# Value bias through the output projection, V copied out by ScalarE, a contiguous residual sum, one-launch maxima, and another order of steps

## The chip, the core and the metric

One NeuronCore of a Trainium2 chip runs the whole program. The metric is the device time of one execution in microseconds (us). Engines are named as in the profile: PE (TensorE), DVE (VectorE), ACT (ScalarE), POOL (GpSimd), SP (SyncE, which here only issues DMAs).

## What is computed

A decoder layer with three parts, each followed by a layer norm, on x of 8 sequences by 128 tokens by 512 features, in float32:

```
x = layernorm(x + self_attention(x))       # 32 heads of 16, qkv and output projections with biases
x = layernorm(x + cross_attention(x, ctx)) # 32 query heads on 8 key/value heads, ctx 8x128x128, additive mask
x = layernorm(x + ffn(x))                  # router softmax over 8 experts scales inputs and outputs of one sign(weight) matmul
# self-attention, as in the reference:
qkv = x @ attn_qkvw + attn_qkvb
probs = softmax(q @ k.T / sqrt(16)); ctx = probs @ v
return ctx @ attn_ow + attn_ob
```

## The kernel before

The eight sequences are worked on in four pairs, i = 0 to 3, each with sequences b = 0 and 1. Three threads of steps are woven into one list, `ORDER`: thread A is self-attention, B is cross-attention and the FFN, C is the set-up of the weights. A token such as `B2.s:0,3` is thread B, pair 2, step `s`, sequence 0, group 3. Every engine walks the same list and does its own part of each step, so the list fixes the order on each engine's queue; across engines only semaphores order the work. The list was written out as a table. PSUM is two rings of banks, one for thread A and one for B and C (class `Ring`): three banks of each rotate over the steps, the fourth is for `pv`. A step on PE waits until the bank it gets has been emptied.

Products that need float32 precision are made of high and low parts: `project` issues three matmuls for each of four slices (`L877` to `L879`). Steps of thread A, in their order of work: `lc`/`xb` load c_in and x_in and make xb = x + output bias on POOL (`L495`); `xt` transposes x; `q:0` to `q:3` make the parts of q and k, each split by ACT (`L575`), DVE (`L695`, `L700`) and POOL (`L501`) and stored to DRAM by SP; `ldq`, `ldk` load them back in a stacked layout (`L336`); `v` projects V, and DVE adds the value bias while it copies it out of PSUM (`L707`); `s` makes scores, of which DVE takes the row maxima (`L713`); `mt` splits those maxima on POOL (`L470` to `L476`), transposes them on PE (`L934`), copies them out on DVE (`L719`) and has SP write them into three rows of the q tile by three DMAs (`L419`); `st` makes the scores transposed with the maxima subtracted (`L943`), ACT takes exp (`L587`); `pv` multiplies by V (`L956`); `ot`, `ct`, `op` normalise, transpose and project (`L738` adds xb to the projection's PSUM bank on DVE), `n1` is the norm. The columns of the features are kept in another order after the norm ("tile-permuted": within each of four tiles, dimension before head), so `L738` writes with a stride.

Thread B has the same steps on the other side: `cp`, `ctx`, `ldc` for the keys, `xt`, `ldx` for the queries, `s` with maxima of score plus mask. Here DVE does one fused operation for each of four 128-column pieces of a bank (`L777`), which writes a full 128x128 result, that nobody reads, over `x2`, and its minimum to `nmb`. From the second group on it first waits for its own previous group to be done:

```
if g > 0:
    rb.wait_emptied(dve, i, "s", b, g - 1)
```

Then follow `st` (`L1010`, `L1011`, `L1013`, exp `L595`), `pv` (`L1021`), `ot`, `n2`, `cx`, and the router and FFN (`rl`, `rt`, `rr`, `is`, `os`, `ff`, `n3`). Set-up steps of thread C: `small` (biases and gate weights), `w` (split of the qkv weight), `ow` (ACT makes owH, `L659`, POOL makes owL, `L550`), `sign`/`swt`, `mask`, `scales`, `rows`.

Of the kernel before, what the change touches and what calls it, by code (L numbers as in the profile page):

```python
# [40 lines left out]
def steps(table):  # L41
# [14 lines left out]
    C0.swt:2 A0.st:1,0 A0.ot:0,1 A0.st:1,1 A0.st:1,2 A0.pv:1,0 A0.ct:0 A0.pv:1,1 A0.pv:1,2 C0.swt:0 A0.st:1,3 C0.rows
    B0.ldc:0 A0.st:1,4 A0.op:0 A0.pv:1,3 A0.st:1,5 A0.st:1,6 A0.pv:1,4 A0.st:1,7 A0.pv:1,5 A0.pv:1,6 A0.pv:1,7 A0.n1:0
    A0.ot:1,0 B0.ldc:1 B0.xt:0 B0.ldx:0 A0.ot:1,1 A1.q:0 A0.ct:1 A1.q:1 A1.q:2 A1.ldq:0 A1.q:3 A0.op:1 B0.s:0,0 A1.v:0
    B0.s:0,1 B0.s:0,2 B0.s:0,3 B0.s:0,4 A1.ldk:0 B0.s:0,5 B0.s:0,6 B0.s:0,7 A1.ldq:1 A0.n1:1 A1.v:1 B0.mt:0 A1.s:0,0
    A1.s:0,1 A1.s:0,2 A1.ldk:1 A1.s:0,3 A1.s:0,4 B0.xt:1 A1.s:0,5 A1.s:0,6 A1.s:0,7 B0.ldx:1 B0.st:0,0 B0.st:0,1  # L60
# [1043 lines left out]
```

## Time and profile before

| | us |
|---|---|
| median of 3 runs | 401.22 (400.49 to 401.77) |
| the profiled execution, its own time | 400.77 |
| its span, first to last instruction | 399.0 |
| PE busy in the span | 336.9 (84%) |
| DVE busy | 263.7 (66%) |
| ACT, POOL busy | 154.5 (39%), 113.2 (28%) |

Matmuls are pipelined and their ends are modelled, so busy PE is not PE at its peak. The granted clock (PEclk) is the share of TensorE's full speed that the throttle let through; a mean of 0.5 in a stretch is its lower level throughout.

### The profile page before, as it was taken

What the parts mean: (1) busy time and instruction counts of PE and PEld (TensorE: products, weight loads), DVE (VectorE), ACT (ScalarE), POOL (GpSimd) and SP (SyncE); (2) the same over time, 40 slices, a digit from 0 to 9 for tenths busy, and PEclk for the clock granted to TensorE, in tenths of its full rate; (3) what the DMA queues carried; (4) which work ended last, traced back from release to release, by engine and by line L of the source; (5) the groups of instructions that cost most, each with busy time, mean ns of one, the idle gap of its engine ahead of it and who ended that gap; (6) DMA issues with size and microseconds to landing.
All of it is one profiled execution on the core that took longest, in us unless ns stands there. A gap on an engine that the chain in (4) does not pass through costs nothing.

```text
span 399.0 us, 7582 instructions
## 1 busy us (share of the span) xinstructions
PE 336.9 (84%) x2661; PEld 240.7 (60%) x2661; DVE 263.7 (66%) x942; ACT 154.5 (39%) x301; POOL 113.2 (28%) x203
## 2 busy tenths in 40 slices
PE   1693789997889999997999999969999977599583
PEld 1692556795647767975567579756556654344251
DVE  1977744558856747698786477977963776933525
ACT  3942145420144854302277642122556611036330
POOL 3363400131240214432432044253022243000231
PEclk9998559998895999997999999967999996569858
DMA  7969700268570000785620016767100053300001
GB/s 270 382 187 250 170 5 5 69 186 222 147 189 4 14 21 25 224 231 145 177 71 2 3 44 194 233 147 194 36 17 1 2 142 109 92 3 2 0 0 53
DMA packets 26702, 42.58 MB, mean 107 GB/s; under 512 B 8153, under 2 KB 18529, under 8 KB 24361
## 3 DMA queue, kind: packets, MB, share of 16 engines
q1 hardware_dynamic: 26393, 41.58, 37.1%
q8 instruction: 21, 0.34, 0.4%
q10 hardware_dynamic: 272, 0.52, 0.3%
q14 instruction: 16, 0.13, 0.1%
HBM read 29.32 MB, written 12.32 MB: 104 GB/s over the span
## 4 chain that ended last, share of the span: by engine, by line
PE 64%; DVE 20%; DMA 5%; issue 4%; ACT 2%; POOL 2%; SPq 2%; POOLq 0%; DVEq 0%; ACTq 0%
DVE x L777 8%; PE bank_a L877 7%; PE bank_a L879 6%; PE bank_a L878 6%; PE bank_a L956 4%; PE bank_a L926 4%; PE bank_b L1021 4%; PE bank_b L1010 4%; PE bank_a L943 3%; PE bank_b L1013 3%; PE bank_b L1011 3%; DVE nma L713 3%; PE bank_b L1056 2%; PE bank_b L1057 2%; PE bank_b L998 2%
## 5 line engine op out<-in xcount | busy, mean ns | idle before, releaser
L777 DVE CUSTOM_DVE_ANT_0 x<-bank_b,mraw 128x128 f32<-128x128 f32 x256 | 59.0, 286 | 8.6 <-PE bank_b L998 2.5
L595 ACT ACTIVATE pb<-bank_b 128x512 f32<-128x512 f32 x64 | 37.6, 600 | 59.7 <-PE bank_b L1013 42.5
L587 ACT ACTIVATE pa<-bank_a 128x512 f32<-128x512 f32 x64 | 37.5, 597 | 25.6 <-PE bank_a L943 13.5
L713 DVE TENSOR_REDUCE nma<-bank_a 128x4 f32<-128x512 f32 x64 | 39.9, 681 | 6.4 <-PE bank_a L926 6.2
L877 PE MATMUL bank_a<-xH,wH 128*128 128x256 f32 x128 | 37.2, 290 | 3.4 <-DVE xL L685 3.4
L1010 PE MATMUL bank_b<-idr,mH 128*128 128x512 f32 x64 | 36.2, 566 | 0.6 <-DVE nmb L777 0.5
L878 PE MATMUL bank_a<-xL,wH 128*128 128x256 f32 x128 | 36.5, 286 | 0.0
L879 PE MATMUL bank_a<-xH,wL 128*128 128x256 f32 x128 | 36.5, 285 | 0.0
L998 PE MATMUL bank_b<-kx,qx 96*128 96x128 bf16 x256 | 26.9, 252 | 11.0 <-DVE nmb L777 8.2
L926 PE MATMUL bank_a<-ks,qs 96*128 96x128 bf16 x256 | 25.2, 250 | 10.6 <-DMA ks<-scr_k 8.4
L998 PEld LDWEIGHTS bank_b<-kx,qx 96*128 96x128 bf16 x256 | 18.4, 112 | 20.4 <-DVE nmb L777 12.4
L926 PEld LDWEIGHTS bank_a<-ks,qs 96*128 96x128 bf16 x256 | 18.8, 112 | 18.4 <-issue 10.3
L956 PE MATMUL bank_a<-pa,va 128*32 128x128 f32 x512 | 27.2, 309 | 0.9 <-ACT wide_a L602 0.4
L877 PEld LDWEIGHTS bank_a<-xH,wH 128*128 128x128 f32 x128 | 24.8, 194 | 3.9 <-DVE xL L685 3.8
L1011 PE MATMUL bank_b<-idr,mL 128*128 128x512 f32 x64 | 26.2, 409 | 0.0
L1013 PE MATMUL bank_b<-qx,kx 99*128 99x512 bf16 x64 | 26.1, 408 | 0.0
L943 PE MATMUL bank_a<-qs,ks 99*128 99x128 bf16 x256 | 25.2, 242 | 0.9 <-DVE nma L713 0.9
L878 PEld LDWEIGHTS bank_a<-xL,wH 128*128 128x128 f32 x128 | 24.8, 194 | 0.0
L879 PEld LDWEIGHTS bank_a<-xH,wL 128*128 128x128 f32 x128 | 24.7, 193 | 0.0
L943 PEld LDWEIGHTS bank_a<-qs,ks 99*128 99x128 bf16 x256 | 17.7, 108 | 8.8 <-issue 6.8
L777 DVE DVE_READ_ACCUMULATOR2_ANT nmb<- 128x1 f32 x256 | 21.1, 82 | 0.0
L481 POOL TENSOR_SCALAR rsb<-mvb 128x1 f32<-128x1 f32 x16 | 3.8, 235 | 58.3 <-DVE mvb L673 58.3
(159 smaller groups left out, 728.3 us busy)
## 6 DMA issues: line engine op xcount, KB each, us to landing
wraw<-in_L_attn_attn_qkvw_dram SPq DMA_DIRECT2D x3, 1024.0 KB, 8.6
scr_q<-qp SPq DMA_DIRECT2D x8, 384.0 KB, 3.1
qs<-scr_q SPq DMA_DIRECT2D x8, 384.0 KB, 4.5
scr_k<-kp SPq DMA_DIRECT2D x8, 384.0 KB, 4.2
ks<-scr_k SPq DMA_DIRECT2D x8, 384.0 KB, 4.8
scr_x<-xp SPq DMA_DIRECT2D x8, 384.0 KB, 2.6
qx<-scr_x SPq DMA_DIRECT2D x8, 384.0 KB, 4.3
qs<-scr_q SPq DMA_DIRECT2D x8, 256.0 KB, 4.7
```

Source lines behind the costliest of these rows:

```text
L713: dve.tensor_reduce(nma[:, b, 4 * j:4 * j + 4], pa_bank(i, *step)[:].rearrange("p (m t) -> p m t", m=KT), AX.X, ALU.max, negate=True).then ...
L777: last = dve.tensor_tensor_reduce(x2[:, b, r * P:(r + 1) * P], pb_bank(i, *step)[:, r * P:(r + 1) * P], mraw[:], -1.0, -LOWEST, ALU.add, A ...
L877: pe.matmul(dst, lh, rh, start=kt == 0, stop=False)
L878: pe.matmul(dst, lh, rl_, start=False, stop=False)
L879: last = pe.matmul(dst, ll, rh, start=False, stop=kt == KT - 1)
L926: last = pe.matmul(dst[:, m * P:(m + 1) * P], qs[0:SR, b, j, m, :], ks[0:SR, b, j, m, :], start=True, stop=True)
L943: last = pe.matmul(dst[:, m * P:(m + 1) * P], ks[0:SM, b, j, m, :], qs[0:SM, b, j, m, :], start=True, stop=True)
L956: last = pe.matmul(dst[m * VW:(m + 1) * VW, (j % 4) * P:(j % 4 + 1) * P], va[:, b, j * KT + m, :], pa[:, n % NP, m * P:(m + 1) * P], start ...
L998: last = pe.matmul(dst[:, r * P:(r + 1) * P], qx[0:SR, b, 4 * (g % 2) + r, g // 2, :], kx[0:SR, b, g, :], start=True, stop=True)
L1010: pe.matmul(d4, mH[:], ident4, start=True, stop=False)
L1011: pe.matmul(d4, mL[:], ident4, start=False, stop=False)
L1013: pe.matmul(d4, kx[0:SM, b, g, :], qx[0:SM, b, a:a + 4, g // 2, :], start=False, stop=True).then_inc(*rb.is_full(i, *step))
```

## The change

1. The value bias is no longer added to V. As the probabilities of a row sum to one, it passes through the attention unchanged, so it is multiplied once by the output weight (a new step `C0.vb`, twelve 128x512 matmuls on PE with the bias column broadcast) and added once to the output bias by DVE. It is loaded as a 4x128 tile (`vraw`) and split in `scales`.
2. V is copied out of PSUM by ACT.
3. The columns of owH and owL are stored tile-permuted, xb is written tile-permuted by POOL, and the residual sum on DVE reads and writes contiguously.
4. The unread result of the fused maxima is written as bfloat16, so that two groups fit into `x2`, and each group waits for the one before the last instead of the last.
5. The three DMAs of a step `mt` become one.
6. `ORDER` is another list, with `C0.vb` added.

```diff
-    A0.lc C0.small C0.w:0 A0.xt:0 A0.xt:1 C0.w:1 C0.w:2 B0.cp:0 B0.cp:1 A1.lc A0.xb A0.q:0 C0.sign A0.q:1 A0.q:2
...
+    C0.small C0.w:0 A0.xt:0 A0.xt:1 C0.w:1 C0.w:2 A0.q:0 C0.sign A0.lc A0.q:1 A0.ldq:0 A0.q:2 C0.swt:3 A0.q:3 A0.ldk:0
...
+            sp.dma_start(vraw[:], qkvb[2 * H:3 * H].rearrange("(t p) -> t p", p=P)).then_inc(ld_small, 16)
-            sp.dma_start(vbias[:], qkvb[2 * H:3 * H].partition_broadcast(P)).then_inc(ld_vb, 16)
...
-                    for c in range(NPART):
-                        row = dst[SR + c:SR + c + 1, b]
-                        sp.dma_start(row.rearrange("r h m t -> r (h m) t"),
-                                     src[c * HEADS:(c + 1) * HEADS, b, :]).then_inc(done, 16)
+                    sp.dma_start(dst[SR:SM, b].rearrange("r h m t -> r (h m) t"), src[:, b, :]).then_inc(done, 16)
...
                     if i == 0:
-                        pool.wait_ge(ld_ob, 16)
+                        rb.wait_emptied(pool, 0, "vb")
...
-                        pool.tensor_tensor(xb[:, b, :], x_in[:, b, :], obias[:], ALU.add).then_inc(xb_made, 1)
+                        pool.tensor_tensor(by_dim(xb[:, b, :]), by_head(x_in[:, b, :]).rearrange("p m h d -> p m d h"),
+                                           by_head(obias[:]).rearrange("p m h d -> p m d h"), ALU.add).then_inc(xb_made, 1)
...
-                        pool.tensor_tensor(owL[:, kt, :], oraw[:, kt, :], owH[:, kt, :].bitcast(F32), ALU.subtract).then_inc(ow_low, 1)
+                        pool.tensor_tensor(by_dim(owL[:, kt, :]), by_head(oraw[:, kt, :]).rearrange("p m h d -> p m d h"),
+                                           by_dim(owH[:, kt, :].bitcast(F32)), ALU.subtract).then_inc(ow_low, 1)
...
+                elif thread == "A" and name == "v":
+                    b = step[1]
+                    ra.wait_full(act, i, *step)
...
+                    act.activation(va[:, b].rearrange("p (h m) w -> p m h w", m=KT)[:, :, :, 0:HD],
+                                   pa_bank(i, *step)[:].rearrange("p (m h d) -> p m h d", m=KT, d=HD), ACT.Copy).then_inc(*ra.is_empty(i, *step))
...
-                        act.activation(owH[:, kt, :], oraw[:, kt, :], ACT.Copy).then_inc(ow_high, 1)
+                        act.activation(by_dim(owH[:, kt, :]), by_head(oraw[:, kt, :]).rearrange("p m h d -> p m d h"), ACT.Copy).then_inc(ow_high, 1)
...
-                elif thread == "A" and name == "v":
...
-                    dve.tensor_tensor(va[:, b].rearrange("p (h m) w -> p m h w", m=KT)[:, :, :, 0:HD],
-                                      pa_bank(i, *step)[:].rearrange("p (m h d) -> p m h d", m=KT, d=HD),
-                                      vbias[:].rearrange("p (m h d) -> p m h d", m=KT, d=HD), ALU.add).then_inc(*ra.is_empty(i, *step))
...
-                    dve.tensor_tensor(tile_permuted(x1[:, b, :]), by_head(pa_bank(i, *step)[:]), by_head(xb[:, b, :]), ALU.add).then_inc(*ra.is_empty(i, *step))
+                    dve.tensor_tensor(x1[:, b, :], pa_bank(i, *step)[:], xb[:, b, :], ALU.add).then_inc(*ra.is_empty(i, *step))
...
-                    if g > 0:
-                        rb.wait_emptied(dve, i, "s", b, g - 1)
+                    unread = x2[:, b, :].bitcast(BF16)
+                    if g > 1:
+                        rb.wait_emptied(dve, i, "s", b, g - 2)
...
-                        last = dve.tensor_tensor_reduce(x2[:, b, r * P:(r + 1) * P], pb_bank(i, *step)[:, r * P:(r + 1) * P], mraw[:], -1.0, -LOWEST,
+                        part = 4 * (g % 2) + r
+                        last = dve.tensor_tensor_reduce(unread[:, part * P:(part + 1) * P], pb_bank(i, *step)[:, r * P:(r + 1) * P], mraw[:], -1.0, -LOWEST,
                                                         ALU.add, ALU.min, nmb[:, b, col:col + 1])
...
+                elif thread == "C" and name == "vb":
+                    rb.wait_full(dve, 0, "vb")
+                    dve.wait_ge(ld_ob, 16)
+                    dve.tensor_tensor(by_head(obias[:]), tile_permuted(pb_bank(i, "vb")[:]), by_head(obias[:]), ALU.add).then_inc(*rb.is_empty(i, "vb"))
                 elif thread == "C" and name == "scales":
+                    dve.wait_ge(vb_split, 1)
+                    dve.tensor_copy(vbH[:], bqk[:, 2 * KT:3 * KT]).then_inc(vb_split, 1)
+                    dve.wait_ge(vb_split, 2)
+                    dve.tensor_tensor(vbL[:], bqk[:, 2 * KT:3 * KT], vbH[:].bitcast(F32), ALU.subtract).then_inc(vb_split, 1)
...
+                elif thread == "C" and name == "vb":
+
+                    rb.wait_free(pe, 0, "vb")
+                    pe.wait_ge(vb_split, 3)
+                    pe.wait_ge(ow_low, KT)
+                    project(pb_bank(i, "vb")[:], lambda kt: (vbH[:, kt:kt + 1].broadcast_to([P, P]), vbL[:, kt:kt + 1].broadcast_to([P, P])),
+                            lambda kt: (owH[:, kt, :], owL[:, kt, :])).then_inc(*rb.is_full(i, "vb"))
```

The order on PE at the start, from the last matmul of the V projection to the first scores (`ks`, `qs` are the stacked keys and queries). Before:

```order
L878 MATMUL bank_a<-wL,xH 128x512
L879 MATMUL bank_a<-wH,xL 128x512
L990 MATMUL bank_b<-idf,c_perm 128x128 [waits c_permuted1]
L926 MATMUL bank_a<-ks,qs 128x128 [waits k_stacked0,q_stacked0,empty_a2]
L926 MATMUL bank_a<-ks,qs 128x128 x3
```

In the change, the first and last rows of the twelve of `vb` among them:

```order
L893 MATMUL bank_a<-wL,xH 128x512
L894 MATMUL bank_a<-wH,xL 128x512
L892 MATMUL bank_b<-owH,vbH 128x512 [waits ow_low,vb_split,empty_b2]
L893 MATMUL bank_b<-owL,vbH 128x512
...
L893 MATMUL bank_b<-owL,vbH 128x512
L894 MATMUL bank_b<-owH,vbL 128x512
L941 MATMUL bank_a<-ks,qs 128x128 [waits k_stacked0,q_stacked0,empty_a2]
```

The first scores now stand behind the bias product, and that behind POOL's four owL passes.

The order on POOL at the start, in the change (the q and k splits came last before, behind the context copies and xb; the owL passes came after both cp operations):

```order
L506 TENSOR_TENSOR qp<-wide_a,qp 128x2x256 [waits a_second] x2
L506 TENSOR_TENSOR kp<-wide_a,kp 128x2x256 [waits a_second] x2
L530 COPY c_perm<-c_in 128x128 [waits ones_b,c_loaded]
L531 COPY vx<-c_in 128x8x16
L530 COPY c_perm<-c_in 128x128 [waits ones_b,c_loaded]
L531 COPY vx<-c_in 128x8x16
L555 TENSOR_TENSOR owL<-oraw,owH 128x512 [waits ow_high]
L555 TENSOR_TENSOR owL<-oraw,owH 128x512 x3
L520 TENSOR_TENSOR cp<-rc,cp 128x128 [waits c_second0]
```

The owL passes moved ahead of the context's third parts, and behind the four context copies.

The order of SP's DMAs ahead of the last pair's cross-attention scores (`qx` queries, `kx` keys). Before:

```order
L370 DMA scr_x<-xp 128x3x512 [waits b_third0]
L336 DMA qx<-scr_x 48x4096 [waits ln_b0,x_stored0]
L336 DMA qx<-scr_x 32x4096
L336 DMA qx<-scr_x 16x4096
L336 DMA kx<-scr_c 48x1024 [waits pv_b,c_stored1]
L336 DMA kx<-scr_c 32x1024
L336 DMA kx<-scr_c 16x1024
L336 DMA kx<-scr_c 48x1024 [waits pv_b,c_stored0]
L336 DMA kx<-scr_c 32x1024
L336 DMA kx<-scr_c 16x1024
```

In the change:

```order
L388 DMA scr_c<-cp 128x3x128 [waits c_third0]
L342 DMA kx<-scr_c 48x1024 [waits pv_b,c_stored0]
L342 DMA kx<-scr_c 32x1024
L342 DMA kx<-scr_c 16x1024
L376 DMA scr_x<-xp 128x3x512 [waits b_third0]
L342 DMA qx<-scr_x 48x4096 [waits ln_b0,x_stored0]
L342 DMA qx<-scr_x 32x4096
L342 DMA qx<-scr_x 16x4096
```

The keys of sequence 0 are loaded before its queries are stored; those of sequence 1 come after.

## Rows read from the trace of the kernel before

**Rows 1.** The page: busy times of the engines, and the chain by line.

```profile
PE 336.9 (84%) x2661; PEld 240.7 (60%) x2661; DVE 263.7 (66%) x942; ACT 154.5 (39%) x301; POOL 113.2 (28%) x203
...
DVE x L777 8%; PE bank_a L877 7%; PE bank_a L879 6%; PE bank_a L878 6%; PE bank_a L956 4%; PE bank_a L926 4%; PE bank_b L1021 4%; PE bank_b L1010 4%; PE bank_a L943 3%; PE bank_b L1013 3%; PE bank_b L1011 3%; DVE nma L713 3%; PE bank_b L1056 2%; PE bank_b L1057 2%; PE bank_b L998 2%
```

**Rows 2.** Windows: start:end, length, busy PE, PEld, DVE, ACT, POOL, PEclk, DMA share, GB/s.

```profile
90.00:100.00 10.00, 7.42 (x49) 5.53 (x47) 9.02 (x60) 0.00 (x0) 1.52 (x3) 0.80 0.81 215
120.00:130.00 10.00, 10.00 (x107) 7.07 (x106) 7.18 (x62) 4.45 (x8) 0.00 (x0) 0.50 0.02 5
180.00:190.00 10.00, 7.39 (x46) 5.45 (x45) 8.09 (x28) 2.34 (x6) 2.38 (x5) 0.73 0.60 147
260.00:270.00 10.00, 6.87 (x42) 5.24 (x40) 7.50 (x31) 2.45 (x6) 4.39 (x8) 0.66 0.63 158
340.00:350.00 10.00, 5.51 (x39) 3.53 (x40) 8.97 (x77) 0.00 (x0) 0.92 (x4) 0.50 0.25 66
```

**Rows 3.** Timeline of DVE: a group's border, a sequence's border, the last piece.

```profile
98.49 0.28 DVE L777 CUSTOM_DVE_ANT_0 x<-bank_b,mraw 128x128 f32<-128x128 f32 x1
98.70 0.28 DVE L777 CUSTOM_DVE_ANT_0 x<-bank_b,mraw 128x128 f32<-128x128 f32 x1
99.14 0.29 DVE L777 CUSTOM_DVE_ANT_0 x<-bank_b,mraw 128x128 f32<-128x128 f32 x1
...
344.25 0.28 DVE L777 CUSTOM_DVE_ANT_0 x<-bank_b,mraw 128x128 f32<-128x128 f32 x1
344.51 0.29 DVE L777 CUSTOM_DVE_ANT_0 x<-bank_b,mraw 128x128 f32<-128x128 f32 x1
...
352.70 0.28 DVE L777 CUSTOM_DVE_ANT_0 x<-bank_b,mraw 128x128 f32<-128x128 f32 x1
```

**Rows 4.** Groups by line and shape: the operations moved or reshaped, and their like.

```profile
L707 DVE TENSOR_TENSOR va<-bank_a,vbias 128x512 f32<-128x512 f32 x8 | 5.5, 687 | 2.3 <-PE bank_a L879 2.2
L738 DVE TENSOR_TENSOR x<-bank_a,xb 128x512 f32<-128x512 f32 x8 | 8.9, 1118 | 7.2 <-PE bank_a L879 7.2
L731 DVE TENSOR_TENSOR cL<-bank_a,cH 128x512 fp32r<-128x512 f32 x8 | 5.5, 686 | 8.2 <-ACT cH L613 8.2
```

**Rows 5.** The last pair's start: DMA issues (KB, us to land), timelines of SP, PE.

```profile
qx<-scr_x SPq DMA_DIRECT2D x8, 384.0 KB, 4.3
...
323.95 1.78 SPq L336 DMA_DIRECT2D qx<-scr_x  x3
325.83 3.71 SPq L336 DMA_DIRECT2D kx<-scr_c  x6
...
331.58 1.15 PE L998 MATMUL bank_b<-kx,qx 96*128 96x128 bf16 x8 [0.35 <-DMA kx<-scr_c]
...
333.49 0.63 PE L1056 MATMUL bank_b<-swT,zH 128*128 128x512 f32 x1
333.91 0.63 PE L1057 MATMUL bank_b<-swT,zL 128*128 128x512 f32 x1
```

**Rows 6.** Timeline of the start: POOL, DVE and PE around the first scores.

```profile
29.65 1.16 POOL L501 TENSOR_TENSOR kp<-wide_a,kp 128x512 bf16<-128x512 f32 x1 [1.67 <-DVE kp L700]
38.50 4.93 POOL L550 TENSOR_TENSOR owL<-oraw,owH 128x512 fp32r<-128x512 f32 x4
...
41.53 4.36 PE L926 MATMUL bank_a<-ks,qs 96*128 96x128 bf16 x32 [8.39 <-DMA ks<-scr_k]
```

**Rows 7.** Timeline of POOL: context copies at the start and in a later pair.

```profile
14.54 0.94 POOL L525 COPY c_perm<-c_in 128x128 f32<-128x128 f32 x1 [10.11 <-DMA c_in<-in_ctx_dram]
16.40 1.15 POOL L525 COPY c_perm<-c_in 128x128 f32<-128x128 f32 x1
...
117.94 0.39 POOL L525 COPY c_perm<-c_in 128x128 f32<-128x128 f32 x1 [3.98 <-PE bank_b L1021]
118.27 0.29 POOL L526 COPY vx<-c_in 128x128 f32<-128x128 f32 x1
```

**Rows 8.** The tile mra: SP's issues, ns min/median/max, first and last start.

```profile
L419 SPq DMA_DIRECT2D qs<-mra x24: 502/590/1359, 49.5 to 289.6; - x24
```

More of the change, by code:

```diff
@@ L56 @@
[L56 to L60, printed above, removed]
@@ L96 @@
-    B3.st:1,4 B3.pv:1,0 B3.st:1,5 B3.st:1,6 B3.st:1,7 B3.ot:1,0 B3.n2:0 B3.pv:1,1 B3.cx:0 B3.ot:1,1 B3.rl:0 B3.rt:0
-    B3.n2:1 B3.cx:1 B3.rl:1 B3.rr:0 B3.rt:1 B3.is:0 B3.rr:1 B3.os:0 B3.is:1 B3.ff:0 B3.os:1 B3.ff:1 B3.n3:0 B3.n3:1
+    C0.small C0.w:0 A0.xt:0 A0.xt:1 C0.w:1 C0.w:2 A0.q:0 C0.sign A0.lc A0.q:1 A0.ldq:0 A0.q:2 C0.swt:3 A0.q:3 A0.ldk:0
+    A0.ldq:1 B0.cp:0 B0.cp:1 A0.ldk:1 C0.ow A0.v:1 C0.scales B0.ctx:0 C0.mask C0.swt:2 B0.ctx:1 A0.v:0 C0.vb A0.s:0,0
+    A0.s:0,1 A0.s:0,2 A0.s:0,3 A0.s:0,4 A0.s:0,5 A0.s:0,6 A0.s:0,7 C0.swt:0 C0.swt:1 A0.mt:0 A0.s:1,0 A0.s:1,1 A0.s:1,2
@@ new lines @@
+    A0.s:1,3 A0.st:0,0 A0.s:1,4 C0.rows A0.s:1,5 A0.st:0,1 A0.s:1,6 A1.lc A0.pv:0,0 A0.s:1,7 A0.xb A0.st:0,2 A0.pv:0,1
+    A0.st:0,3 A0.st:0,4 A0.pv:0,2 A0.pv:0,3 A0.mt:1 A0.st:0,5 B0.ldc:1 A0.st:0,6 A0.pv:0,4 A0.st:0,7 A0.pv:0,5 A1.xt:0
+    A0.pv:0,6 A0.pv:0,7 A0.st:1,0 A0.ot:0,0 A0.ot:0,1 A0.st:1,1 A0.st:1,2 A0.pv:1,0 A0.ct:0 A0.pv:1,1 A0.st:1,3
+    A0.st:1,4 A0.pv:1,2 A0.pv:1,3 A0.op:0 A0.st:1,5 A0.pv:1,4 A0.st:1,6 A0.st:1,7 A0.ot:1,0 B0.ldc:0 A0.n1:0 A0.pv:1,5
+    A1.xt:1 A0.pv:1,6 A0.pv:1,7 B0.xt:0 B0.ldx:0 A0.ot:1,1 A1.q:0 A1.q:1 A1.ldq:0 A0.ct:1 A1.q:2 A1.q:3 A1.ldk:0 A0.op:1
@@ L98 @@
+    B3.s:1,0 B3.s:1,1 B3.s:1,2 B3.mt:0 B3.s:1,3 B3.s:1,4 B3.s:1,5 B3.s:1,6 B3.s:1,7 B3.st:0,0 B3.st:0,1 B3.st:0,2
+    B3.st:0,3 B3.mt:1 B3.st:0,4 B3.pv:0,0 B3.st:0,5 B3.st:0,6 B3.st:0,7 B3.ot:0,0 B3.st:1,0 B3.pv:0,1 B3.st:1,1
+    B3.st:1,2 B3.st:1,3 B3.ot:0,1 B3.st:1,4 B3.pv:1,0 B3.st:1,5 B3.st:1,6 B3.st:1,7 B3.ot:1,0 B3.pv:1,1 B3.n2:0 B3.cx:0
+    B3.ot:1,1 B3.rl:0 B3.rt:0 B3.rr:0 B3.n2:1 B3.cx:1 B3.is:0 B3.rl:1 B3.rt:1 B3.rr:1 B3.os:0 B3.is:1 B3.ff:0 B3.os:1
+    B3.ff:1 B3.n3:0 B3.n3:1
 """)
@@ L165, in decoder_layer @@
         ocS = sb("ocS", [4 * E, H], F32R)
-        bqk = sb("bqk", [P, 2 * KT], F32)
-        vbias = sb("vbias", [P, H], F32)
+        bqk = sb("bqk", [P, 3 * KT], F32)
+        vbH = sb("vbH", [P, KT], F32R)
+        vbL = sb("vbL", [P, KT], F32R)
         obias = sb("obias", [P, H], F32)
@@ L304, in by_head, with by_dim @@
             return ap.rearrange("p (m h d) -> p m h d", m=KT, d=HD)
+        def by_dim(ap):
+            return ap.rearrange("p (m d h) -> p m d h", m=KT, d=HD)
         def tile_permuted(ap):
```

97 lines of the change are left out of this document (46 added, 51 removed).

## The prediction

> **What bounds the kernel now.** I read the page first: PE is busy 84% of the span, DVE 66%, and the largest single entry of the chain that ended last is DVE's fused maxima, 8% of 399 us, about 32 us [rows 1]. Neither engine bounds the whole. At the start PE waits 8.39 us for the reloaded keys, up to 41.53 [rows 6]. The windows show who bounds what after that [rows 2]. In each pair comes a stretch in which the maxima of both attentions fall together: DVE is busy 9.02 of 10 us at 90 to 100 while PE has 2.58 us idle; the same pattern costs PE 2.61 us at 180 to 190 and 3.13 us at 260 to 270. In the last pair there is no self-attention left to fill in, and PE is idle 4.49 us of the 10 at 340 to 350 with DVE at 8.97. Elsewhere PE is full. So DVE work is worth its time in those stretches, and nearly nothing outside them.
>
> The timeline of DVE then shows something inside its work [rows 3]. Pieces of one group start 0.21 us apart (98.49, 98.70). The next group's first piece starts 0.44 us after the last piece (98.70 to 99.14), although its scores are in. That border is where DVE waits for its own previous group. At 344.25 to 344.51 the border between two sequences, where there is no such wait, takes 0.26 us. So the wait costs about 0.2 us a border.
>
> **The change, part by part.**
>
> *The wait for the group before the last.* With the bfloat16 result, the semaphore waited for is one group (0.86 us) old. I take each border down from 0.44 to 0.22 us, a gain of 0.22 us. The fused operation reads PSUM and float32 either way, so its own 0.28 us I leave; bounds for its change of output type are 0 by the row of its like, nothing nearer being shown. In a dense stretch of the middle pairs six borders follow each other directly (others have another DVE operation between): 1.3 us.
>
> The Trainium skill, "VectorE: DVE Perf Modes", section "The DRAIN you can't avoid", says the opposite: eight copies with a semaphore after each took as long as eight with one at the end, so the semaphore costs nothing extra. By that, this part is worth zero. It is a rival below.
>
> *V out by ScalarE.* It takes 0.69 us from DVE eight times [rows 4], two of them in each dense stretch: 1.4 us. On ACT, idle for all of 90 to 100 us [rows 2], it hides; if ACT were busy with exp when V arrives, PE's bank would be held for one exp longer.
>
> *Contiguous residual.* 1.118 us becomes what the contiguous like takes, 0.686 us [rows 4], 0.43 us each, eight times; one of them falls in each dense stretch. The price is a strided sum on POOL, with two inputs read by stride. POOL is busy 28% and xb is needed much later, so it hides, except where the new list puts it directly ahead of the split of the maxima (pair 1): there it is covered by eight reductions of the scores.
>
> So a dense stretch of a middle pair loses 1.3 + 1.4 + 0.4 = 3.1 us of DVE. PE's idle time in the middle one is 2.61 us, and it can't gain more than it idles; I take 2.6 us for each of the three: **7.8 us**. Bounds: 1.8 without the border term, 3.1 with all of it.
>
> *The last pair.* From 331.58 [rows 5] to 352.98 us [rows 3] DVE works through the last sixteen groups, 64 pieces, with thirteen such borders: 13 x 0.22 = **2.9 us**, all on the path, since PE stands idle 4.49 us in the middle of it even at its lower clock, 0.50 granted [rows 2]. Its first scores wait for the keys of sequence 0, the last of six DMAs that SP issues at 325.83 for 3.71 us, behind three for the queries [rows 5]. In the new list those keys come first. Late next are the queries: the last of three is issued at about 325.1 and, with the usual 4.3 us to land [rows 5], is there at about 329.5, and PE has other steps to do before the scores until 331.2, so I take **1.2 us**, bounds 0.4 (the wait shown) to 3.7 (the issues).
>
> *One DMA for the maxima.* Two issues of 0.59 us less on SP [rows 8], sixteen times. The bytes are the same. It is on the path only where PE has nothing else while it waits for `st`: at the start. I take 1.2 us there and 0 elsewhere, where PE's other thread covers it (PE is 10.00 busy at 120 to 130, [rows 2]). A slower single DMA, spread over fewer transfers, would show in the same place; bound 1 us the other way.
>
> *The start, where the change costs.* One more small DMA ahead of the weights: the first split waits for it, 0.4 us. Then the bias product: the first scores stand behind it on PE, and it behind POOL. POOL ends the last key split at 30.81 [rows 6]. Four context copies follow: 1.4 us if quiet (0.39 and 0.29 each), 4.1 us if slowed as at the start, when DVE had two-input work beside them (0.94 to 1.15) [rows 7]; the new list has DVE's `scales` there, so I take 3 us: 33.8. The four owL passes took 4.93 us, 1.23 each [rows 6]. With one input by stride I add the difference of the strided copy to the plain one, 0.10 us for 128 columns, so 0.4 for 512: 4 x 1.66 = 6.6 us, up to 40.5. Twelve 128x512 matmuls after an idle PE, as the FFN's after the idle PE of the last pair, start 0.42 us apart [rows 5]: 5.1 us, up to 45.6, against 41.53 now. That is 4.1 us, and DVE's sum of the bias, like the strided 1.1 us, delays the first maxima by another 0.6. Bounds: 37.1 + 2.8 (full clock) = 39.9, so no delay at all; or 35 + 10 + 5.1 = 50.1, 8.6 us. Given back: 1.2 us by the single DMA, and 1.0 us because DVE has less ahead of the first `mt` copy: two casts instead of a cast and two subtractions of 0.69 us [rows 4] with their waits. Start: 0.4 + 4.1 + 0.6 - 1.2 - 1.0 = **+2.9 us**.
>
> On owL the Trainium skill, "GPSIMD Engine Reference", section "Performance pitfalls for Q7 kernels", gives +50% for reads with a step above 8 bytes. It would make a pass 1.85 us (an estimate from that page and the 1.23) and the start 0.8 us later than my sum; no row here shows a strided two-input pass.
>
> *Sum:* -7.8 - 2.9 - 1.2 + 2.9 = -9.0 us. The profiled execution has 400.77 us; the median of the runs is 0.45 higher. 401.22 - 9.0 = **392.2 us**. The rest of the new list moves steps by a few places where PE is full; I cost it at nothing, covered by PE's queue of the other thread. If that cover fails, new idle time of the size of the old (1 to 3 us a stretch) appears.
>
> **Rivals.**
> - *Borders are free* (the page's rule). For it: the measurement that the page reports. Against: the 0.26 us border without the wait. It takes 3 x 1.3 (of which 0.5 in all was capped anyway) and 2.9 us back: 392.2 + 6.3 = 398.5. Chance 0.08.
> - *Gains turn into other waits.* DVE comes earlier, but PE waits for reloads, whose DMA share is 0.81 in these stretches [rows 2], or for reordered steps. Half of the 7.8 and 2.9 goes: 397.5. For it: SP and the DMA engines are busiest there. Chance 0.15; the upper third of it is no change.
> - *The clock pays more.* Now 120 to 130 us runs at 0.50 granted with PE 10.00 busy [rows 2]: some 5 us lost. If the stalls shrink enough that the lower level doesn't follow, up to 5 us there and 2 us after 260: 386. Chance 0.19.
> - *Slower: POOL's strided passes hold the start.* If a strided two-input pass is slowed as the context copies were (1.15 against 0.39 us, times 2.9), it takes 3.6 us: 35 + 14.4 + 5.1 = 54.5, 13 us late, and xb's two passes ahead of the split in pair 1 stick out by 3. With 0.6 + 0.4 and the 2.2 given back that is 14.8 us against 11.9 gained: 404. It turns the sign from about 2.9 us a pass on. For it: DVE has two-input work beside POOL's at the start again. Against: the four owL passes took 1.23 each without such work beside them, and `scales` ends before they begin. Chance 0.12.
> - *Not as said:* the same-type neighbour rows mislead and nothing changes within 0.3%: 0.03.
>
> **How the numbers follow.** My forecast has 0.43, in its own range 388 to 396; it rests on borders and V, both on rows. 0.3% (1.2 us) is about what a measurement can tell from no change. Faster by more than that: 0.43 + 0.19 + 0.07 + 0.11 = 0.80; the same 0.07 (the last case and parts of two others); slower 0.13. The range runs from 384 (clock case, with a little more) to 402, leaving out most of the slower case.
>
> **What would show it.** Borders of `L777`'s successor at 0.22 us, and its groups at 0.86; PE idle in 90 to 120 below 3 us; V copies on ACT at about 0.6 us; the residual at 0.69; PE's first scores at 44 to 47 us, with the bias product right before; POOL's owL passes at 1.7 us; the last pair's scores some 9 us earlier. It is wrong if the borders stay at 0.44, if the first scores come later than 50 us, or if the span shrinks while the dense stretches don't.

## The result and the profile after

The changed kernel takes **415.91 us** (median of 4 runs, 413.12 to 417.69), the kernel before beside it 400.86: 1.037 times as long, 95% interval 1.030 to 1.043. The forecast was 392.2, the range 384 to 402; the sign was wrong, and so was the range. The profiled execution took 416.56 us, its span is 414.5 (before 400.77 and 399.0). Ratios, here and below, are of the fast runs alone against those of the kernel before beside them (two of e2's four and two of e11's six runs were slow), so they can differ by some us from what the medians give.

The page of the changed kernel: busy times, and two groups of section 5 (line, engine, operation, tiles, busy and mean ns, then the idle time before it and what ended it).

```profile
PE 340.8 (82%) x2674; PEld 241.3 (58%) x2674; DVE 258.5 (62%) x937; ACT 159.9 (39%) x309; POOL 120.8 (29%) x203
...
L784 DVE CUSTOM_DVE_ANT_0 x<-bank_b,mraw 128x128 bf16<-128x128 f32 x256 | 55.5, 287 | 12.5 <-DMA out_dram<-x 11.4
...
L1013 PE MATMUL bank_b<-kx,qx 96*128 96x128 bf16 x256 | 27.9, 255 | 23.4 <-DVE nmb L784 21.1
```

DVE has 5.2 us less to do than in [rows 1] and still everything ends later. The second line is new: before its maxima DVE sat idle 11.4 us for `out_dram`, the store of the layer's output. In the trace of before no instruction waits for that store. The third says who paid: PE waited 21.1 us for the maxima (`L998` in the kernel before: 8.2 us). Of the 15.5 us by which the span is longer, PE is busy for 3.9 and idle for 11.6. The mean granted clock of the two profiled executions is the same (0.885, before 0.881), so a lower clock is not the cause.

The groups of the moved and reshaped operations in the changed kernel, against [rows 4] and [rows 6]:

```profile
L590 ACT ACTIVATE va<-bank_a 128x512 f32<-128x512 f32 x8 | 4.8, 594 | 29.6 <-PE bank_a L894 29.6
...
L742 DVE TENSOR_TENSOR x<-bank_a,xb 128x512 f32<-128x512 f32 x8 | 5.5, 689 | 10.9 <-PE bank_a L894 10.9
...
L499 POOL TENSOR_TENSOR xb<-x_in,obias 128x512 f32<-128x512 f32 x8 | 15.7, 1979 | 0.0
L555 POOL TENSOR_TENSOR owL<-oraw,owH 128x512 fp32r<-128x512 f32 x4 | 7.2, 1838 | 0.0
```

V on ScalarE takes 0.59 us and the residual 0.69, as forecast. The strided passes on POOL take 1.84 us (`L555`, one input by stride) and 1.98 us (`L499`, both), where I took 1.66 for the first.

**Where it went.** I lay both traces side by side by the first write of `nmb` in each sequence, the first cross maximum (`L777`, now `L784`). In pair 0 it stands at 92.4 us before and 95.4 after: +3.0. The lag then stands at +5.4 (pair 0, sequence 1), +4.3 and +4.5 (pair 1), **+14.5** (pair 2, sequence 0, at 265.3), +13.5, **+17.5** (the last pair, at 350.2), +15.0 (its second sequence) and +15.5 at the end. Two jumps, then, and a slow loss beside them.

The timelines of SP and of DVE in the changed kernel at the first jump, and DVE's line at the second (start, duration, engine, line):

```profile
256.50 0.90 SPq L350 DMA_DIRECT2D scr_q<-qp  x2
259.09 1.77 SPq L342 DMA_DIRECT2D qs<-scr_q  x3
260.91 0.58 SPq L447 DMA_DIRECT2D out_dram<-x  x1
```

```profile
255.37 1.40 DVE L691 TENSOR_SCALAR x<-x,mvb,rsb 128x512 f32<-128x512 f32 x1
...
260.22 0.43 DVE L713 CAST kp<-wide_a 128x512 bf16<-128x512 f32 x1
265.08 0.29 DVE L784 CUSTOM_DVE_ANT_0 x<-bank_b,mraw 128x128 bf16<-128x128 f32 x1 [4.44 <-DMA out_dram<-x]
...
349.94 0.29 DVE L784 CUSTOM_DVE_ANT_0 x<-bank_b,mraw 128x128 bf16<-128x128 f32 x1 [4.77 <-DMA out_dram<-x]
```

The unread result of the maxima lies in `x2`, so a pair's first group of a sequence waits until the output of the pair before has been stored from there. In the new list the normalisation that makes this output stands behind the next pair's first query split, and SP issues the store behind the query stores and reloads: at 260.91. DVE is done with everything else at 260.65 and idles 4.44 us, and since it works in order, the maxima of the self-attention behind it wait as well. In the list before, SP issued the same store at 244.99, 5.6 us ahead of the maxima that need it.

DVE waits for the store three times: 2.21 us from 205.7, 4.44 from 260.6 and 4.77 from 345.2. The windows of the changed kernel around the first two, columns as in [rows 2]:

```profile
200.00:210.00 10.00, 8.06 (x93) 5.03 (x89) 7.41 (x24) 5.18 (x10) 2.42 (x8) 0.99 0.21 57
210.00:220.00 10.00, 9.61 (x94) 5.99 (x87) 8.79 (x44) 4.11 (x8) 6.09 (x5) 0.50 0.26 84
260.00:270.00 10.00, 4.66 (x34) 3.04 (x32) 5.39 (x36) 0.27 (x1) 3.73 (x5) 0.89 0.87 260
270.00:280.00 10.00, 9.29 (x36) 7.03 (x36) 5.98 (x44) 1.70 (x5) 4.17 (x6) 0.60 0.03 6
```

PE's idle time may be paid twice here. Behind the window at 200 to 210 us, in which PE is idle 1.94 us, it is 9.61 busy from 210 to 220 at a granted clock of 0.50, the lower level, 1.2 GHz: by my estimate some 5 us more for the same work. The kernel before had such a stretch too, in another place (120 to 130, [rows 2]), where the changed kernel ran at 1.00; over the whole span the two cancel.

### The profile page after: what moved, and what is told of

Its sections match the earlier page's. It is cut to its first block, busy times and chain, and to the rows that moved or that the text cites. A ratio compares the mean times of both kernels' runs of the same rounds, so it can differ in the third digit from the quotient of the medians.

```text
span 414.5 us, 7580 instructions
## 1 busy us (share of the span) xinstructions
PE 340.8 (82%) x2674; PEld 241.3 (58%) x2674; DVE 258.5 (62%) x937; ACT 159.9 (39%) x309; POOL 120.8 (29%) x203
## 4 chain that ended last, share of the span: by engine, by line
PE 62%; DVE 18%; DMA 7%; issue 5%; POOL 4%; ACT 2%; SPq 1%; POOLq 0%; DVEq 0%; ACTq 0%
PE bank_a L892 7%; DVE x L784 7%; PE bank_a L894 7%; PE bank_a L893 6%; PE bank_b L1025 4%; PE bank_a L971 4%; PE bank_b L1026 4%; PE bank_b L1028 4%; PE bank_b L1036 3%; PE bank_a L958 3%; PE bank_a L941 3%; PE bank_b L1071 2%; DVE nma L717 2%; DMA out_dram<-x 2%; PE bank_b L1072 2%
## 5 line engine op out<-in xcount | busy, mean ns | idle before, releaser
L784 DVE CUSTOM_DVE_ANT_0 x<-bank_b,mraw 128x128 bf16<-128x128 f32 x256 | 55.5, 287 | 12.5 <-DMA out_dram<-x 11.4
L1013 PE MATMUL bank_b<-kx,qx 96*128 96x128 bf16 x256 | 27.9, 255 | 23.4 <-DVE nmb L784 21.1
L717 DVE TENSOR_REDUCE nma<-bank_a 128x4 f32<-128x512 f32 x64 | 40.1, 683 | 3.9 <-PE bank_a L941 3.6
L958 PE MATMUL bank_a<-qs,ks 99*128 99x128 bf16 x256 | 24.2, 234 | 2.8 <-issue 1.6
L941 PE MATMUL bank_a<-ks,qs 96*128 96x128 bf16 x256 | 21.9, 231 | 1.5 <-DVE nma L717 1.5
L784 DVE DVE_READ_ACCUMULATOR2_ANT nmb<- 128x1 f32 x256 | 21.5, 84 | 0.0
L941 PEld LDWEIGHTS bank_a<-ks,qs 96*128 96x128 bf16 x256 | 17.2, 103 | 6.3 <-DVE nma L717 2.7
```

The lines of the kernel that those rows point to most:

```text
L717: dve.tensor_reduce(nma[:, b, 4 * j:4 * j + 4], pa_bank(i, *step)[:].rearrange("p (m t) -> p m t", m=KT), AX.X, ALU.max, negate=True).then ...
L784: last = dve.tensor_tensor_reduce(unread[:, part * P:(part + 1) * P], pb_bank(i, *step)[:, r * P:(r + 1) * P], mraw[:], -1.0, -LOWEST, ALU ...
L941: last = pe.matmul(dst[:, m * P:(m + 1) * P], qs[0:SR, b, j, m, :], ks[0:SR, b, j, m, :], start=True, stop=True)
L958: last = pe.matmul(dst[:, m * P:(m + 1) * P], ks[0:SM, b, j, m, :], qs[0:SM, b, j, m, :], start=True, stop=True)
L1013: last = pe.matmul(dst[:, r * P:(r + 1) * P], qx[0:SR, b, 4 * (g % 2) + r, g // 2, :], kx[0:SR, b, g, :], start=True, stop=True)
```

## The experiments

**Which part costs: the list or the code?** Theory L says the list of steps, rival C the edits of the code. e1 gives the code before the whole new list, all but its entry C0.vb:

```diff
-    A0.lc C0.small C0.w:0 A0.xt:0 A0.xt:1 C0.w:1 C0.w:2 B0.cp:0 B0.cp:1 A1.lc A0.xb A0.q:0
+    C0.small C0.w:0 A0.xt:0 A0.xt:1 C0.w:1 C0.w:2 A0.q:0 C0.sign A0.lc A0.q:1 A0.ldq:0 A0.q:2
 ...
```

> The kernel before with the changed kernel's list of steps (less the bias product, which it has not): no other edit. Theory L (the list is what costs): about 411 us, since in the changed kernel some 10 us went between 200 and 265 us and 3.5 before the last pair, none of it in an operation that got longer; DVE's first group of a pair then waits for the output's store as in the changed kernel. Rival C (the code's edits cost, the list is neutral): 400 to 402 us.

431.17 us (430.83 to 434.31), ratio 1.086 (1.078 to 1.093). The new list alone costs 31 us by the medians (34 by the ratio), three times what I expected, and the code's edits win some 15 of it back (19 by the ratios). The wait for the store is there too, 11.8 us, three times.

e2 and e3 keep the changed code, and its list up to one entry (e2: A0.op:1, e3: A1.op:1); behind that come all other entries in the order of the old list. For e2:

```diff
     A1.xt:1 ... A1.q:3 A1.ldk:0 A0.op:1
-    B0.s:0,0 B0.s:0,1 B0.s:0,2 B0.s:0,3 B0.s:0,4 B0.s:0,5 B0.s:0,6 B0.s:0,7 A0.n1:1 A1.v:0
+    B0.s:0,0 A1.v:0 B0.s:0,1 B0.s:0,2 B0.s:0,3 B0.s:0,4 B0.s:0,5 B0.s:0,6 B0.s:0,7 A1.ldq:1
 ...
```

> The changed code with its own list up to the last output projection of pair 0, and from there the order of the kernel before. Theory L: the start costs its 3 us, the edits gain in the dense stretches, so 394 to 400 us. Rival C: stays at 413 to 418 us.

397.96 us (391.65 to 401.02), ratio 0.990 (0.979 to 1.000), which rests on two runs.

> The changed code with its own list up to the last output projection of pair 1, then the order of the kernel before. Theory L with the loss in the steps of pair 2 (200 to 265 us): 398 to 404 us, near e2. If the loss is laid earlier, in the list's steps of pair 1: 410 or more. Rival C: 413 to 418 us.

401.93 us, ratio 1.007 (1.002 to 1.011). Rival C has fallen. In the share of the time before, the list's steps between the two switches, in pairs 0 and 1, cost 1.7% (e3 against e2, whose intervals nearly touch) and those behind them 3.0% (changed kernel against e3). One wait for the store, of 1.4 us, is in e3's trace too.

**Is the border real?** e4 is the changed kernel with the old wait:

```diff
-                    if g > 1:
-                        rb.wait_emptied(dve, i, "s", b, g - 2)
+                    if g > 0:
+                        rb.wait_emptied(dve, i, "s", b, g - 1)
```

> The changed kernel, but DVE's group of maxima waits for the group before it again (g - 1), all else as changed. If the border costs 0.2 us and DVE's dense stretches are on the path: the first pieces of groups 0.44 apart from the piece before again, and 6 to 8 us slower than the changed kernel, 422 to 424 us. If DVE's time is not on the path of the changed kernel: 414 to 418 us.

425.72 us, ratio 1.071 (1.064 to 1.078): 10 us slower than the changed kernel by the medians, 14 by the ratios, and so more than the 6 to 8 I had expected. Two of DVE's pieces in e4 with a border between them, and under them five pieces in a row of the changed kernel's last pair; with four pieces a group, a border lies among them:

```profile
375.24 0.28 DVE L784 CUSTOM_DVE_ANT_0 x<-bank_b,mraw 128x128 bf16<-128x128 f32 x1
375.68 0.29 DVE L784 CUSTOM_DVE_ANT_0 x<-bank_b,mraw 128x128 bf16<-128x128 f32 x1
```

```profile
363.19 0.29 DVE L784 CUSTOM_DVE_ANT_0 x<-bank_b,mraw 128x128 bf16<-128x128 f32 x1
363.40 0.29 DVE L784 CUSTOM_DVE_ANT_0 x<-bank_b,mraw 128x128 bf16<-128x128 f32 x1
363.61 0.29 DVE L784 CUSTOM_DVE_ANT_0 x<-bank_b,mraw 128x128 bf16<-128x128 f32 x1
363.82 0.29 DVE L784 CUSTOM_DVE_ANT_0 x<-bank_b,mraw 128x128 bf16<-128x128 f32 x1
364.03 0.29 DVE L784 CUSTOM_DVE_ANT_0 x<-bank_b,mraw 128x128 bf16<-128x128 f32 x1
```

The border takes 0.44 us with the wait for one group and 0.21 without, as much as any step from piece to piece: no border is left. So most of the 15 to 19 us that the code's edits won in e1's comparison is this one edit.

**Is it the store?** e5 takes away what makes DVE wait, e6 moves the store back:

```diff
+        unr = sb("unr", [P, 8 * P], BF16)
...
-                    unread = x2[:, b, :].bitcast(BF16)
+                    unread = unr[:]
...
-                    elif i > 0:
-
-                        dve.wait_ge(out_stored[b], 16 * i)
+                    elif b > 0:
+                        rb.wait_emptied(dve, i, "s", b - 1, g + HT - 2)
+                    elif i > 0:
+                        rb.wait_emptied(dve, i - 1, "s", GB - 1, g + HT - 2)
...
+                    if u == 0 and i > 0:
+                        dve.wait_ge(out_stored[b], 16 * i)
                     dve.tensor_tensor(x2[:, b, :].rearrange("p (u c r d) -> p u r c d", u=2, c=4, d=HD)[:, u], v[:, :, :, 0:HD],
```

> The changed kernel and list, but the unread result of the maxima goes into a buffer of its own, so that only the later writer of x2 waits for the output's store. Theory S (the store is what the new list put in front of DVE): DVE's three waits for it, 2.2 + 4.4 + 4.8 = 11.4 us, vanish and with them most of PE's idle time there, so 400 to 407 us. Rival P (the list packs the cross scores so that PE waits for DVE, the store's wait only lies beside that): 411 to 416 us, and the waits turn into others.

406.79 us (404.99 to 409.62), ratio 1.020 (1.012 to 1.027).

```diff
-    A2.s:0,7 B1.st:0,3 B1.st:0,4 B1.st:0,5 A2.s:1,0
+    A2.s:0,7 B1.st:0,3 B1.st:0,4 B1.st:0,5 B0.n3:1 A2.s:1,0
-    A2.st:0,0 A2.st:0,1 B1.pv:0,1 B0.n3:1 B1.s:1,0
+    A2.st:0,0 A2.st:0,1 B1.pv:0,1 B1.s:1,0
-    A2.ct:1 A3.q:1 A3.ldq:0 B1.n3:0 B1.n2:1
+    A2.ct:1 B1.n3:0 A3.q:1 A3.ldq:0 B1.n2:1
-    B2.rr:1 A3.n1:1 B3.ctx:1 B3.ldc:1 B2.is:1 B3.xt:1 B2.n3:0 B3.s:0,0 B2.os:1
+    B2.rr:1 B2.n3:0 A3.n1:1 B3.ctx:1 B3.ldc:1 B2.is:1 B3.xt:1 B2.os:1 B3.s:0,0
```

> The changed code, its list with four entries moved: the last normalisation with its store of sequence 1 of pair 0 (B0.n3:1), of sequence 0 of pair 1 and of pair 2 (B1.n3:0, B2.n3:0) earlier, and the first scores of the last pair (B3.s:0,0) behind the FFN's output. Theory S: 398 to 406 us, no wait of DVE for the store. Rival P: 411 to 416 us.

405.88 us (404.28 to 407.94), ratio 1.017 (1.011 to 1.023). Two different ways of taking the same wait away give the same time, and in both traces no instruction of DVE waits for the store. So the store's wait is worth 9 to 10 us of the changed kernel's median, 7 to 8 by the ratios. More than half of the list's cost, though, is something else: e6 is still over the kernel before.

**The start, and the list before in full.** e7 has the changed code and the old list with the bias product put behind the first scores:

```diff
-    B0.cp:1 A1.lc A0.xb A0.q:0
+    B0.cp:1 A1.lc A0.q:0
-    A0.s:0,7 C0.swt:3 A1.xt:0 A1.xt:1 A0.mt:0
+    A0.s:0,7 C0.vb C0.swt:3 A0.mt:0
-    A0.s:1,6 A0.s:1,7 A0.st:0,1
+    A0.s:1,6 A0.s:1,7 A0.xb A0.st:0,1
-    A0.pv:0,5 A0.ot:0,0
+    A0.pv:0,5 A1.xt:0 A0.ot:0,0
-    A0.pv:1,4 A0.st:1,7
+    A0.pv:1,4 A1.xt:1 A0.st:1,7
```

> The changed code with the list of the kernel before; added is the bias product behind the first sequence's self-attention scores instead of ahead of them, and the residual's sum (A0.xb) and the next x transposes (A1.xt) behind it. If the start's cost is the product ahead of the first scores: these come at 41 to 43 us and the whole takes 389 to 394 us. If the start costs the same wherever the product stands: 396 to 400 us, as with the list that switches after pair 0.

393.0 us (389.55 to 393.59), ratio 0.983 (0.976 to 0.989). The first scores come at 41.66 us: the product costs nothing ahead of them. The first cross maximum comes at 94.9 us, 2.8 behind e8's 92.1. That isn't shown to be the product's price: e10 below, which has no product, has it at 94.5. The changed code with this list, nearly the old one, is 3.4% faster than the same code with e6's list and 5.2% faster than the changed kernel (by the ratios).

**What of the gain is the border's?** e8 is the kernel before with that edit alone:

```diff
-                    if g > 0:
-                        rb.wait_emptied(dve, i, "s", b, g - 1)
+                    unread = x2[:, b, :].bitcast(BF16)
+                    if g > 1:
+                        rb.wait_emptied(dve, i, "s", b, g - 2)
...
-                        last = dve.tensor_tensor_reduce(x2[:, b, r * P:(r + 1) * P], ...
+                        part = 4 * (g % 2) + r
+                        last = dve.tensor_tensor_reduce(unread[:, part * P:(part + 1) * P], ...
```

> The kernel before with one edit: the maxima's unread result in bfloat16 in halves, and the wait for the group before the last. The border theory as predicted: borders 0.44 to 0.22 us, 1.3 us in each of three dense stretches and 2.9 us in the last pair, 6 to 7 us faster than the kernel before, 393 to 395 us. If borders cost nothing: 399 to 401 us.

391.75 us (391.06 to 393.04), ratio 0.982 (0.976 to 0.989): 7.2 us faster, just above what I had expected. The two profiled executions lie further apart, 9.8 us (spans of 399.0 and 389.2). Where? The windows of e8 (its maxima of pair 0, sequence 1, begin at 118.4), and then two stretches from the first cross maximum of one sequence to that of the next, of e8 and of the kernel before:

```profile
120.00:130.00 10.00, 9.99 (x166) 7.13 (x164) 9.16 (x57) 7.75 (x15) 0.91 (x4) 1.00 0.03 7
...
118.40:165.20 46.80, 46.79 (x466) 36.42 (x464) 33.78 (x130) 26.30 (x53) 13.40 (x23) 1.00 0.25 72
...
244.60:275.90 31.30, 28.75 (x189) 20.50 (x188) 26.53 (x105) 6.68 (x14) 10.95 (x19) 0.84 0.68 181
```

```profile
120.20:171.00 50.80, 50.79 (x468) 39.23 (x466) 34.34 (x128) 26.43 (x53) 13.41 (x23) 0.90 0.22 60
...
250.80:282.90 32.10, 28.65 (x190) 20.28 (x189) 26.68 (x103) 6.68 (x14) 10.93 (x19) 0.84 0.66 176
```

The dense stretch of pair 2 is only 0.8 us shorter, PE's idle time in it 2.55 us instead of 3.45. The large piece, 4.0 of the 9.8 us, is in the stretch behind the first dense one, where PE never idled: it ran 120 to 130 us at 0.50 in the kernel before [rows 2] and at 1.00 here. My clock rival said this, for 5 us. That the edit brings it about isn't shown, since these are single executions, and the same kernel's differ: beside e8, the kernel before took 396.5 and 396.7 us where its mean granted clock was 0.897 and 0.901, and e8 391.3 and 391.1 at 0.896 and 0.901. So 5 to 6 us of the gain are there at equal mean clock.

**Is the packing of the cross scores the rest?** e9 is e6 with the eight scores of pair 0, sequence 1, spread as in the old list:

```diff
-    A1.pv:0,3 B0.s:1,0 B0.s:1,1 B0.n2:0 A1.st:0,6 ... B0.s:1,2 A1.mt:1 ... B0.s:1,7 A1.st:1,0
+    B0.s:1,0 B0.s:1,1 A1.st:0,0 ... B0.s:1,2 B0.s:1,3 A1.pv:0,0 ... B0.s:1,6 B0.s:1,7 A1.pv:0,4
```

> The changed kernel with the four entries moved as in e6_stores_earlier, and besides the eight cross scores of sequence 1 of pair 0 (B0.s:1,0 to 7) spread among the exp groups of the other thread (A1.st, A1.pv) as in the list of the kernel before; in the changed list they stand late, packed beside steps that need DVE. Theory P (this packing is the second cost: from the first cross maxima of pair 0 to those of pair 1 e6 takes 80.1 us, e7 with the old list 72.5): 398 to 401 us. Rival: the loss there comes from other steps of pair 0 and 1, 404 to 407 us.

409.26 us (407.69 to 410.55), ratio 1.022 (1.018 to 1.026): nothing gained, and slower than either theory had it, so theory P falls in this form. PE's idle time from there to the next pair's maxima does shrink (from 4.09 to 1.63 us), but just before, the scores now wait 1.57 us for their reload (`qx<-scr_x`), and PE's granted clock is down between 122 and 137 us (0.66, 0.50 and 0.81 in three windows of 5). What the trace of e6 shows instead is many small waits in stretches where e7 has none. The same two stretches in e6 and in e7:

```profile
127.00:176.80 49.80, 45.71 (x414) 34.99 (x414) 30.73 (x124) 22.52 (x47) 15.74 (x27) 1.00 0.28 77
207.70:259.60 51.90, 47.59 (x458) 35.92 (x459) 34.45 (x126) 25.05 (x52) 18.37 (x27) 1.00 0.24 69
```

```profile
120.70:167.40 46.70, 46.69 (x467) 36.37 (x464) 33.32 (x128) 26.32 (x53) 13.40 (x23) 1.00 0.23 66
199.30:246.30 47.00, 46.97 (x469) 35.76 (x466) 32.66 (x127) 26.57 (x54) 13.83 (x27) 1.00 0.23 70
```

0.01 and 0.03 us of PE idle with the old list, 4.09 and 4.31 with the new. PE's largest waits of e6 in the second stretch (line, what it waited for, us in total, times, longest):

```profile
PE bank_b L1041 <- DVE x L690: 1.3, 1, 1.3
PE bank_a L978 <- ACT wide_a L614: 1.1, 2, 0.8
PE bank_b L1004 <- POOL c_perm L529: 0.7, 1, 0.7
PE bank_a L957 <- DVE x L730: 0.4, 1, 0.4
PE bank_b L1024 <- DMA qx<-mrb: 0.3, 1, 0.3
```

Five producers, on DVE, ACT, POOL and the DMA queues: steps that PE reaches a little before their input is ready. No one of them makes up the whole.

**What V on ScalarE, the residual and the single DMA give.** e10 is the changed code with the old list untouched and the bias product left out, so V's bias is missing from its output:

```diff
-    A0.v:0 C0.vb A0.s:0,0
+    A0.v:0 B0.ctx:1 C0.ow A0.s:0,0
...
-                        rb.wait_emptied(pool, 0, "vb")
+                        pool.wait_ge(ld_ob, 16)
```

> The changed code with exactly the list of the kernel before and without the bias product, so without V's bias in the output: what V on ScalarE, the contiguous residual and the single DMA give apart from the start. As predicted for the dense stretches and the last pair (V and residual worth up to 1.8 us each of three): 387 to 390 us, 2 to 5 below e8. Rival N (once the borders are shorter, PE is full there and DVE's saved 9 us are worth nothing): 390.5 to 393 us, as e8.

391.6 us (391.16 to 394.53), ratio 0.979 (0.975 to 0.984), e8's 0.982 (0.976 to 0.989). The intervals overlap and rival N stands: with 9 us of DVE work removed (an estimate, 8 x 0.69 and 8 x 0.43), no gain can be told.

e11 is e8 with the single DMA:

```diff
-                    for c in range(NPART):
-                        row = dst[SR + c:SR + c + 1, b]
-                        sp.dma_start(row.rearrange("r h m t -> r (h m) t"),
-                                     src[c * HEADS:(c + 1) * HEADS, b, :]).then_inc(done, 16)
+                    sp.dma_start(dst[SR:SM, b].rearrange("r h m t -> r (h m) t"), src[:, b, :]).then_inc(done, 16)
```

> e8_only_wait_two_groups and one DMA for the three parts of the maxima instead of three. As predicted: 1.2 us faster than e8 by the start, 390 to 391 us. Rival: the single DMA is slower to land and nothing is gained, 391.5 to 393 us.

392.87 us, but the runs spread from 389.01 to 397.69; ratio 0.979 (0.974 to 0.985). That is inconclusive: 1.2 us is below what this comparison tells. One issue takes 0.78 us where three took 0.59 each [rows 8].

e12 is e11 with one entry moved:

```diff
-    B2.ff:0 B3.ldx:0 A3.op:1 B3.ldc:1 B3.ldc:0 B2.rl:1
+    B2.ff:0 B3.ldc:0 B3.ldx:0 A3.op:1 B3.ldc:1 B2.rl:1
```

> e11_single_dma with one entry of the old list moved: the reload of the keys of the last pair's sequence 0 (B3.ldc:0) ahead of the reload of its queries (B3.ldx:0) on SP. As predicted: the last pair's first scores come 1.2 us earlier, 389 to 390 us. Rival: the queries are then late by as much, the same as e11.

**391.35 us** (387.31 to 393.07), ratio 0.977 (0.971 to 0.982), the lowest ratio of all and 5.8% under the changed kernel's by ratio. In the stretch up to the last pair's first maxima PE idles 3.91 us instead of e11's 6.12, and its wait of 2.56 us for `kx` is gone; the stretch is 0.7 us shorter, at a mean granted clock of 0.94 against 0.97. The whole cannot be told from e11 or e8.

## Why the prediction was wrong

The step that failed is "The rest of the new list moves steps by a few places where PE is full; I cost it at nothing, covered by PE's queue of the other thread." With the changed code it costs what lies between e7 and the changed kernel, 5.4% of 399 us, about 22 us. By the same ratios: the new start 2.8 us (e2 against e7; their intervals overlap, so this may be nothing), the steps of pairs 0 and 1 6.7 (e3 against e2), those behind them without the store's wait 4.3 (e6 against e3), the store's wait 7.9 (changed kernel against e6). I had priced each step's own work and never asked, for each entry moved later, who waits for what it makes. The rule I had set myself (if the cover fails, 1 to 3 us a stretch) had the right mechanism, but at most 9 us for three stretches against the 22, and no rival carried it to the other side.

The rest, step by step:

- *Slower rival.* I had it on POOL's passes at the start. It was one mechanism with the wrong place: the output's store, on SP's queue. The place could have been found: two `n3` entries stand in the new list right ahead of the maxima that overwrite their `x2`.
- *The start, +2.9.* Measured +3.0 at the first cross maximum in the profiled execution, which is luck in part. The first scores come at 46.43 us against my 45.6, 4.9 later than before and not 4.1, and 1.9 of that is regained by the first cross maximum. Other executions with the same steps up to there have it later: 98.6 us in e2, 99.0 in e3 and 98.8 in e5. About 1 us of that stands at their first scores already (47.24 in e2, 47.51 in e3); behind these PE is full from 60 to 70 us at a granted clock of 0.50, where the changed kernel had 0.85. So the start costs 3 to 6.6 us, from one execution to another. The window of the changed kernel, and that of e2:

```profile
60.00:70.00 10.00, 9.45 (x129) 6.15 (x127) 2.93 (x8) 6.59 (x12) 0.91 (x4) 0.85 0.16 46
```

```profile
60.00:70.00 10.00, 10.00 (x106) 6.35 (x105) 2.38 (x5) 5.65 (x11) 0.91 (x4) 0.50 0.24 75
```

  The passes took 1.84 us each where I took 1.66 (1.23 + 0.4 is 1.63). I had `scales` end before they begin; it ran beside them to 40.1 us, and they weren't slowed as the slower rival had it. The Trainium skill, "GPSIMD Engine Reference", section "Performance pitfalls for Q7 kernels", says that reads with a step above 8 bytes take 50% longer, which made 1.85 us a pass as an estimate and the start 0.8 us later than my sum. There the trace agrees with the page to 0.01 us a pass, and not with me; of the 0.8 us at the first scores the passes are 0.6.
- *The borders, 0.44 to 0.22.* Right: 0.21. Alone they bring 7.2 us (e8), and putting them back costs 10 (e4, 14 by the ratios). My price for the rival of free borders was 1.0 us too high: without them each dense stretch still gains 1.8 of its 2.6 us, so 2.4 and 2.9 us are taken back, which makes 397.5. The Trainium skill, "VectorE: DVE Perf Modes", section "The DRAIN you can't avoid", from which I drew the rival that borders are free, measured a semaphore signalled after each copy, and not a wait for it, so the rival does not follow from it. Here such a wait, for the group just issued on the same engine, cost 0.23 us in e4 (0.44 against 0.21).
- *Dense stretches, 3 x 2.6 us.* Wrong in the reading for two of the three, though the sum of the border edit fitted. From a pair's first cross maximum to that of its second sequence e8 is 1.5, 0.3 and 0.9 us shorter than the kernel before, where I had 1.3 each for the borders. I took PE's idle time there for DVE's throughput. That fits pair 0, where PE waits for maxima of the cross scores four times, 2.6 us in all. In pairs 1 and 2 PE's one wait of size in the kernel before is for the router (2.3 and 2.8 us): the transpose of `rts`, behind logits, exp, reciprocal and three small DVE operations, one after the other. In pair 2:

```profile
262.36 0.15 DVE L800 TENSOR_REDUCE nl<-bank_b 128x1 f32<-128x8 f32 x1
262.94 0.16 DVE L805 RECIPROCAL rl<-sl 128x1 f32<-128x1 f32 x1 [0.42 <-ACT el L636]
263.14 0.23 DVE L807 TENSOR_SCALAR rt<-el,rl 128x8 f32<-128x8 f32 x1
263.40 0.17 DVE L811 CAST rts<-rt 128x16 fp32r<-128x16 f32 x1
263.61 0.17 DVE L813 TENSOR_TENSOR rts<-rt,rts 128x16 f32<-128x16 f32 x1
```

```profile
263.93 0.37 PE L1042 MATMUL bank_b<-idf,rts 128*32 128x128 f32 x1 [2.79 <-DVE rts L813]
```

  This chain begins when PE has made the logits, whatever DVE has saved before. In e7, with V and the residual gone from DVE, PE still waits 2.51 us for it, and POOL's strided sum takes part of the saving back:

```profile
256.37 0.17 DVE L806 TENSOR_REDUCE nl<-bank_b 128x1 f32<-128x8 f32 x1 [0.47 <-PE bank_b L1052]
257.10 0.16 DVE L811 RECIPROCAL rl<-sl 128x1 f32<-128x1 f32 x1 [0.56 <-ACT el L648]
257.30 0.91 DVE L813 TENSOR_SCALAR rt<-el,rl 128x8 f32<-128x8 f32 x1
```

```profile
254.26 3.92 POOL L498 TENSOR_TENSOR xb<-x_in,obias 128x512 f32<-128x512 f32 x2
```

- *V and residual, 1.8 us a stretch.* Worth nothing that can be measured (e10).
- *The last pair, 2.9 + 1.2.* From the first cross maximum to the last it takes 20.5 us before and 19.1 in e8: 1.4, not 2.9. Eleven borders of 0.44 us stand there, not thirteen, and none in e8: 2.4 us. Of these 0.9 went into another wait, DVE's for the FFN's product (`L824`, in e8 `L826`), 1.3 us before and 2.2 in e8. Keys first removed the wait for them (e12), and the stretch before lost 0.7 us.
- *The clock.* The rival had 5 us at 120 to 130 us. There the changed kernel, too, ran at 1.00 granted, and so did e8's profiled execution; what brings the lower level about is open. I had not asked whether it would come elsewhere; 210 to 220 us is such a place in the changed kernel.

What stays open: which of the many moved entries of pairs 0 to 2 make up the 11 us that neither the store nor, as far as pair 0 was tried, the packing explains. e9 shows that taking back one group of them is no help by itself, since a new wait and the clock took its place. Open too is what decides the granted clock of a stretch.
